# Reading packed zeros once per bit field, and moving small steps at the start of a dequantising FFN-attention-FFN kernel

## The reference

```python
def _dequant(qweight, scales, qzeros, g_idx):
    shifts = jnp.arange(PACK, dtype=jnp.uint32) * BITS          # PACK = 8, BITS = 4
    w = (qw[:, None, :] >> shifts[None, :, None] & MAXQ).reshape(-1, qweight.shape[1])
    z = ((qz[:, :, None] >> shifts[None, None, :] & MAXQ) + 1).reshape(qzeros.shape[0], -1)
    s = scales[g_idx]
    return (w.astype(scales.dtype) - z[g_idx].astype(scales.dtype)) * s
...
    h = jax.nn.silu(xf @ Wg) * (xf @ Wu)        # 512 -> 1376
    out = h @ Wd                                # 1376 -> 512
...
x = x + 0.5 * _L0_ffn_ref(_layernorm(x, axis=-1), ...)
x = x + _L0_attn_ref(_layernorm(x, axis=-1), ...)
x = x + 0.5 * _L0_ffn_ref(_layernorm(x, axis=-1), ...)
```

## Time and profile before

| | us |
|---|---|
| median of 3 runs | 819.42 (818.62 to 819.49) |
| the profiled execution | 819.34 |
| its span in the trace | 817.5 |
| TensorE busy in the span | 804.9 |
| VectorE / ScalarE / GpSimd busy | 497.4 / 271.3 / 303.5 |

### The profile page before, as it was taken

The page is one execution under the profiler, slowest core; times in us unless marked ns, Lnnn a source line. Parts: engine busy times, 40 slices in busy tenths (PEclk is TensorE's granted clock), DMA queues, the critical chain, the costliest instruction groups (busy, mean ns, idle before and its releaser), DMA issues.

```text
span 817.5 us, 10482 instructions
## 1 busy us (share of the span) xinstructions
PE 804.9 (98%) x3840; PEld 662.1 (81%) x3840; DVE 497.4 (61%) x801; ACT 271.3 (33%) x467; POOL 303.5 (37%) x237
## 2 busy tenths in 40 slices
PE   5999999999999999999999999999999999999998
PEld 4777788878888888788898888888878888888786
DVE  7999945756654543572869895545347743443452
ACT  3433423555211211342765862112124321221221
POOL 5655614751114463237554881055432110110100
PEclk9999999999999999999999999999999999999999
DMA  6999968965755368446366169554867164444131
GB/s 160 299 304 303 322 203 291 339 255 232 262 186 170 129 201 205 112 154 217 76 160 218 40 211 373 188 163 156 223 195 220 53 228 145 140 167 132 29 104 51
DMA packets 102301, 155.62 MB, mean 190 GB/s; under 512 B 51916, under 2 KB 62852, under 8 KB 97258
## 3 DMA queue, kind: packets, MB, share of 16 engines
q1 hardware_dynamic: 95056, 143.26, 54.2%
q10 hardware_dynamic: 6330, 7.47, 2.7%
q0 software_dynamic: 864, 4.23, 1.9%
HBM read 104.30 MB, written 44.27 MB: 182 GB/s over the span
## 4 chain that ended last, share of the span: by engine, by line
PE 93%; DVE 4%; issue 1%; DMA 1%; POOL 0%; ACT 0%; ACTq 0%; DVEq 0%
PE ps L896 44%; PE ps L889 39%; PE ps L951 5%; PE ps L970 2%; PE ps L1301 2%; PE ps L907 1%; DVE wi L1827 1%; DMA sc_gu<-in_L_ffn_up_scales 1%; DVE qs L1919 1%; PE ps L998 0%; DVE pT L1827 0%; DVE mx L2176 0%; DVE wf L1945 0%; DVE xT L1827 0%; ACTq L1637 0%
## 5 line engine op out<-in xcount | busy, mean ns | idle before, releaser
L889 PE MATMUL ps<-blk,ring 128*128 128x512 f32 (+1 forms) x1386 | 320.7, 389 | 0.0
L889 PEld LDWEIGHTS ps<-blk,ring 128*128 128x128 f32 (+1 forms) x1386 | 256.7, 185 | 57.8 <-issue 0.2
L896 PE MATMUL ps<-wd,hT 128*128 128x512 f32 (+1 forms) x963 | 227.7, 391 | 0.1
L896 PEld LDWEIGHTS ps<-wd,hT 128*128 128x128 f32 (+1 forms) x963 | 179.9, 188 | 38.7 <-DVE h L1995 0.5
L2403 POOL TENSOR_TENSOR h<-h,u 128x512 f32<-128x512 f32 (+1 forms) x33 | 42.7, 1294 | 299.4 <-ACT h L1558 299.4
L1830 DVE TENSOR_TENSOR u<-ps,p1s 128x512 f32<-128x512 f32 (+1 forms) x66 | 45.4, 687 | 95.5 <-PE ps L889 95.4
L1558 ACT ACTIVATE h<-h 128x512 f32<-128x512 f32 (+1 forms) x33 | 20.9, 632 | 174.9 <-DVE h L1830 174.9
L1830 DVE TENSOR_TENSOR h<-ps,p1s 128x512 f32<-128x512 f32 (+1 forms) x33 | 22.8, 691 | 64.1 <-PE ps L889 64.1
L1830 DVE TENSOR_TENSOR u<-ps,u 128x512 f32<-128x512 f32 (+1 forms) x66 | 45.6, 691 | 24.5 <-PE ps L889 23.4
L2344 POOL TENSOR_SCALAR xn<-xn,mv,rstd 128x512 f32<-128x512 f32 x28 | 59.0, 2114 | 0.8
L951 PE MATMUL ps<-xT,wp 128*128 128x512 f32 x240 | 58.6, 394 | 0.1
(11 more groups left out here) (145 smaller groups left out, 992.0 us busy)
## 6 DMA issues: line engine op xcount, KB each, us to landing
ring<-wsaved SPq DMA_DIRECT2D x29, 1024.0 KB, 5.2
ring<-wsaved SPq DMA_DIRECT2D x33, 768.0 KB, 4.5
wsaved<-wp SPq DMA_DIRECT2D x10, 1024.0 KB, 4.5
stream<-xres SPq DMA_DIRECT2D x32, 256.0 KB, 2.6
xres<-stream SPq DMA_DIRECT2D x32, 256.0 KB, 4.0
xn<-stream SPq DMA_DIRECT2D x7, 1024.0 KB, 7.3
wfull<-wf ACTq DMA_DIRECT2D x20, 256.0 KB, 4.9
wsaved<-wp SPq DMA_DIRECT2D x10, 512.0 KB, 5.2
```

What stands on the lines that cost most here:

```text
L889: mm = pe.matmul(ps[0:w, bank, :], ring[:, slot, which, a, kt, 0:w], blk[:, which, b, kt, :], start=not onto and kt == 0 and n == 0, stop= ...
L896: mm = pe.matmul(bank_ap, lhs(a), rhs(b), start=first and n == 0, stop=last and n == 2)
```

## The change

1. **Zeros.** The packed words are loaded with each word row on eight partitions (a broadcast over eight in the load), so gate and up take 64 partitions of 172 words and down 80 of 64. One shift by `shift`, a value per partition, replaces the eight shifts. The result lies field by field, so the two readers address it through a rearranged view: the zeros' multiplications of `scales_zeros` step 172 values (344 bytes) from one column to the next and the subtraction for down 64 values (128 bytes). `shift` is the first load of SP's stream, with a semaphore of its own; the zeros' loads follow it.
2. **Order in the head.** `ln_stats(0, (2, 3))` stands ahead of the first `ln_shift`, and the second `ln_shift` stands behind `table_gu` and `unpack(0)`.
3. **Less warming.** `keep_warm(2)` ahead of the first `scales_zeros` is gone, `keep_warm(4)` ahead of `plain_top` becomes `keep_warm(2)`.
4. **Attention, first sequence.** The low parts of the second tile of probabilities and of the values stand ahead of `ln_var(7)` and the low part of the queries; `pv` waits for five of s_qkvlo, and the score of tile 4 for six.

```diff
-            step(*(lambda j=j: eng.tensor_scalar(zi[:, :, j], zq, BITS * j, 15, ALU.logical_shift_right, ALU.bitwise_and)
-                   for j in range(PACK)))
-            step(*(lambda zb=zb, add=add, by=by: eng.tensor_scalar(zb, zi.rearrange("p c j -> p (c j)"), add, by, ALU.add, ALU.mult)
+            step(lambda: eng.tensor_scalar(zi, zq, shift[0:zq.shape[0], 0:1], 15, ALU.logical_shift_right, ALU.bitwise_and))
+            step(*(lambda zb=zb, add=add, by=by: eng.tensor_scalar(zb, zi, add, by, ALU.add, ALU.mult)
                    for zb, add, by in results))
...
+            sp.dma_start(shift[:, :], shifts).then_inc(d_shift, 16)
             for m in range(2):
-                sp.dma_start(zq_gu[m * ZP:(m + 1) * ZP, :], flat(zeros[m], ZC)).then_inc(d_zq_gu, 16)
-            sp.dma_start(zq_d, flat(zeros[2], ZC_D)).then_inc(d_zq_d, 16)
+                words = flat(zeros[m], ZC).rearrange("r (o c) -> r o c", o=1).to_broadcast([ZP, PACK, ZC])
+                sp.dma_start(zq_gu[m * ZP * PACK:(m + 1) * ZP * PACK, :], words).then_inc(d_zq_gu, 16)
+            sp.dma_start(zq_d, zeros[2].rearrange("r (o c) -> r o c", o=1).to_broadcast([GD, PACK, ZC_D])).then_inc(d_zq_d, 16)
...
-            sp.dma_start(shift[:, :], shifts).then_inc(d_small, 16)
...
+            def zeros_of(i, w):
+                words = slice(i * P // PACK, (i * P + w) // PACK)
+                return zb_gu[Z_ROWS, :].rearrange("r (j c) -> r c j", j=PACK)[:, words, :]
...
-                    pe.matmul(ps[:, Z_BANK, k * P:k * P + w], oh_gu[Z_ROWS, cols], zb_gu[Z_ROWS, i * P:i * P + w], start=True, stop=True)
+                    pe.matmul(ps[:, Z_BANK, k * P:k * P + w], oh_gu[Z_ROWS, cols], zeros_of(i, w), start=True, stop=True)
...
                 if r == 2:
-                    keep_warm(2)
...
-            keep_warm(4)
+            keep_warm(2)
...
+                            if j == 2:
+                                pe.wait_ge(s_qkvlo, 6)
...
-                        pe.wait_ge(s_qkvlo, 3 * (2 * b + 2))
+                        pe.wait_ge(s_qkvlo, 5)
...
+                    by_word = unit_view(u, z).rearrange("p (j c) -> p c j", j=PACK)
+                    minus(unit_view(u, wi[:, :]).rearrange("p (c j) -> p c j", j=PACK),
+                          flat.rearrange("p (c j) -> p c j", j=PACK), by_word).then_inc(s_int, 1)
...
+            ln_stats(0, (2, 3))
             ln_shift(0, (0, 1))
-            ln_stats(0, (2, 3))
...
-            ln_shift(0, (2, 3))
...
             unpack(0)
+            ln_shift(0, (2, 3))
...
+                p_lo(b, 1)
+                v_lo(a)
                 ln_var(t)
                 qk_lo(a, 0, qT)
-                p_lo(b, 1)
-                v_lo(a)
```

More of the change, by code:

```diff
@@ L204, in macaron @@
         left_gu = scratch("left_gu", [P, TAB_TILES * P], F32)
-        ZP = 16
-        ZC = GK * INTER // PACK // ZP
-        zq_gu = scratch("zq_gu", [P, ZC], I32)[0:2 * ZP, :]
-        zi_gu = scratch("zi_gu", [P, ZC, PACK], I32)[0:2 * ZP, :, :]
-        zs_gu = [scratch(f"zs_gu{m}", [P, ZC * PACK], BF16)[0:2 * ZP, :] for m in range(2)]
+        ZP = GK
+        ZC = INTER // PACK
+        zq_gu = scratch("zq_gu", [P, ZC], I32)[0:2 * ZP * PACK, :]
+        zi_gu = scratch("zi_gu", [P, ZC], I32)[0:2 * ZP * PACK, :]
+        zs_gu = [scratch(f"zs_gu{m}", [P, ZC], BF16)[0:2 * ZP * PACK, :] for m in range(2)]
         keep = scratch("keep", [P, 2], F32)
-        ZC_D = 8
-        ZP_D = GD * HID // PACK // ZC_D
+        ZC_D = HID // PACK
+        ZP_D = GD * PACK
         zq_d = scratch("zq_d", [P, ZC_D], I32)[0:ZP_D, :]
-        zi_d = scratch("zi_d", [P, ZC_D, PACK], I32)[0:ZP_D, :, :]
-        zb_d = scratch("zb_d", [P, ZC_D * PACK], BF16)[0:ZP_D, :]
+        zi_d = scratch("zi_d", [P, ZC_D], I32)[0:ZP_D, :]
+        zb_d = scratch("zb_d", [P, ZC_D], BF16)[0:ZP_D, :]
         over_blk = placer(blk_at, ring_at)
@@ L305, in macaron @@
         d_zb = sem("d_zb")
+        d_shift = sem("d_shift")
         d_cut_rest = sem("d_cut_rest")
@@ L521, in macaron @@
         FIRST_STEPS, PART_STEPS = 3, 7
-        ZERO_STEPS, ZERO_D_STEPS, TAB_STEPS = PACK + 2, 2 * PACK + 3, 2 * PACK + 4
+        ZERO_STEPS, ZERO_D_STEPS, TAB_STEPS = 3, 5, 6
         FLAT_LOADS, PART_LOADS = 32, 128
         def unpack_zeros(eng, step, zq, zi, *results):
-            step(*(lambda j=j: eng.tensor_scalar(zi[:, :, j], zq, BITS * j, 15, ALU.logical_shift_right, ALU.bitwise_and)
-                   for j in range(PACK)))
-            step(*(lambda zb=zb, add=add, by=by: eng.tensor_scalar(zb, zi.rearrange("p c j -> p (c j)"), add, by, ALU.add, ALU.mult)
+            step(lambda: eng.tensor_scalar(zi, zq, shift[0:zq.shape[0], 0:1], 15, ALU.logical_shift_right, ALU.bitwise_and))
+            step(*(lambda zb=zb, add=add, by=by: eng.tensor_scalar(zb, zi, add, by, ALU.add, ALU.mult)
                    for zb, add, by in results))
@@ L716, in _ @@
             for m, row in enumerate((Z_ROW, Z_UP)):
-                sp.dma_start(zb_gu[row:row + GK, :], zs_gu[m][m * ZP:(m + 1) * ZP, :]).then_inc(d_zb, 16)
+                sp.dma_start(zb_gu[row:row + GK, :], zs_gu[m][m * ZP * PACK:(m + 1) * ZP * PACK, :]).then_inc(d_zb, 16)
             sp.wait_ge(s_cst, 4)
@@ L1195, in turn_pair @@
                 turn_block(q, A12, kt)
-            pe.wait_ge(d_small, 32)
+            pe.wait_ge(d_small, 16)
             keep_warm(3)
@@ L1934, in dequantise @@
                     s, z = ps[:, S_BANKS[m], :], zeros_at(m)
-                minus(unit_view(u, wi[:, :]), flat, unit_view(u, z)).then_inc(s_int, 1)
+                    minus(unit_view(u, wi[:, :]), flat, unit_view(u, z)).then_inc(s_int, 1)
                 dve.wait_ge(s_int, u + 1)
@@ L2141, in _ @@
                 constants(lambda: dve.memset(keep[row:row + 2 * GK, 1:2], 0.0), lambda: dve.memset(keep[row:row + GK, 0:1], 0.0))
+            dve.wait_ge(d_shift, 16)
             dve.wait_ge(d_zq_gu, 32)
@@ L2158, in _ @@
             table_gu(dve, tables)
-            dve.wait_ge(d_small, 32)
             unpack(0)
+            ln_shift(0, (2, 3))
             dequantise(0)
```

## The result

The changed kernel takes 831.12 us (median of five runs, 830.63 to 831.75), the kernel before beside it 818.83 (818.44 to 819.49): a ratio of 1.0148, 95% interval 1.0137 to 1.0160. The forecast was 820.1 with a range to 823.0. The profiled execution took 830.63, its span is 828.7 where before has 817.5.

A forecast was written before the change was run, and what follows sets the result against it. TensorE, busy 804.9 of 817.5 us, was taken as the bound, leaving only its late start and few waits. Head +1.1, attention -0.3, reads and warming 0 gave +0.8 on 819.34: 820.1 us, range 817.9 to 823.0.

The forecast's parts named there:

- The strided reads: TensorE's 44 zeros' products and VectorE's 11 subtractions for down: stepped reads taken at nothing, with 2.4 us on TensorE as upper bound.
- the writing row: VectorE's eight old shifts of `zi_gu`, writing every 32 bytes, took 0.10 us apart for 43 words; read as steps being free.
- The rival that named this mechanism: Strided reads cost double: 2.4 us on TensorE beside the forecast's 0.8, 822.5 us; chance 0.18.
- The landing: When up's zeros arrive and VectorE's unpacking starts: 5.3 us instead of 3.56, bounds 4.1 and 6.3.
- the third load's 3.9 us: Landing time of `zq_d`, third in SP's stream before the change; it says 5.7 for up's zeros, and 5.3 was taken.
- The rest of the chain: Head: unpacking to second `nmr` 7.9 us, then 0.2 + 2.9 until ScalarE's stream is free for the first high part.
- the head's +1.1: ScalarE's first high part goes from 15.20 to 16.3, so TensorE's start and the weights' chain to 40.57 come 1.1 us later.
- Warming: Fewer multiplications ahead of `scales_zeros` and the first product: costed at nothing, since TensorE's four products wait for high parts anyway.
- a rival of 1.4 to 3.2 us: TensorE stays at 1.2 GHz longer for want of warming, 8 to 16 products slower: 822.4 with the rest; chance 0.12.
- Attention: TensorE's 0.42 us wait at 399.01 ends; late `ln_var(7)` delays GpSimd and ScalarE's third scaling, so 0.3 us gain is kept.
- the 1.2 us of VectorE that unpacking frees: One wide shift replaces eight in VectorE's head: 0.72 us freed for the first unpacking, 0.50 for down's.
- VectorE's step of 0.4 us being covered: VectorE's stepped subtraction for down: taken at nothing; upper bound 1.0 us for two down units ahead of 40.57, none hidden.

## Where the prediction was right and where it failed

**The strided reads: the step that failed most.** They were taken at nothing, "by the writing row", with an upper bound of twice the time, 2.4 us. They cost 7.0 to 7.2 us by the times and 5.9 in the trace (6.2 for the ten blocks, less 0.3 for the wait at 40.57, which is gone). The row chosen was a write, on another engine, and says nothing of a read by TensorE; the bound of two had no row behind it, and the factor was nearly four (0.20 for 0.055). The rival that named this mechanism was right in kind and had 0.18, but its price came from the same bound. With 0.15 x 44 = 6.6 added the sum would have been 826.7. The rule weighed beside it (the Trainium skill, "SBUF — State Buffer", section "Door 1: The DMA port swizzle") was right against the row; on TensorE two values to a 16-byte piece, with which it expects full rate, still cost nearly double (0.09 to 0.12 us for 0.055 to 0.07).

**The landing: mis-sized.** 5.3 was forecast, at most 6.3; it was 6.86. The step that failed is the term taken "a little less" than the third load's 3.9 us: from up's issue, at 2.10 and not 1.8, to unpacking it was 4.8. The forecast had weighed that four engines would carry this load, as its four marks bear out, and kept to the row. The rest of the chain held: from unpacking to the second `nmr` 7.84 us (forecast 7.9), from there to ScalarE's free stream 3.14 (3.1), the first high part at 17.88, where the same sum with 6.86 gives 17.86 (its bracket names VectorE's `wf`, but that was done by 17.0 and the stream at 17.84). So the head's +1.1 became 2.7 there by this one number. It is 2.4 at the first product and 2.8 at `scales_zeros(1)`: the four products between them took 2.10 us for 1.68, which no run here takes apart.

**Warming: the wrong case of the two.** It was costed at nothing with a rival of 1.4 to 3.2 us at 0.12. The rival came, 2.5 by the times, 2.0 in the trace. The argument against it was that nine microseconds of small products had not raised the level by 15 us. That is so, but the kernel before then rose at 18.2, just ahead of the 32 products, and some of the multiplications that the change took out were among the work in between; without them the changed kernel rose at 26.7.

**Attention: wrong sign.** The prediction named the very chain (`ln_var(7)` late, GpSimd full, the third scaling) and took 0.1 off for it; it took the whole 0.42 and 0.3 more.

With the four terms as the trace has them the sum nearly closes: 820.1, plus 5.9 for the reads, 1.7 for the head, 2.0 for the clock and 0.6 for the attention is 830.3; the profiled execution took 830.63, the median is 831.12.

**Right:** the 1.2 us of VectorE that unpacking frees (0.70 and 0.43), the small price of the order, and VectorE's step of 0.4 us being covered. The last was right by luck: its cover was TensorE's slowness, which the forecast did not have.

## What to carry to other kernels

A layout that saves a few instructions on an engine with time to spare must be priced by who reads it most often on the engine that has none: count the 16-byte pieces that each read of TensorE touches, and measure one such read if no row shows it. A bound without a row behind it is no bound. Before a step is put behind others, follow what it feeds, over GpSimd and ScalarE back to TensorE; and where a load is the first thing that the head waits for, look at what stands ahead of it in the stream: one more small load cost 1.6 us here, not the 0.5 of its issue. A clock that reads full is worth a check against the durations of equal instructions before a warming is taken out.

## What the chip showed that was not expected

- The zeros' products read bf16 at a price of about 1.6 to 1.8 ns for each 16-byte piece of a row touched; 128 values at steps of 16 to 344 bytes take 0.20 to 0.23 us, at 8 bytes 0.09 to 0.12, at 4 bytes nothing extra, and 0.20 at 1.2 GHz as well (21.41 to 21.61) as at 2.4. VectorE's reads are free up to 8 bytes and cost 0.4 us on 512 values from 16 bytes on.
- The views print a granted clock of 1.00 for the time ahead of a trace's first record, while the products may run at half rate (22.4 to 26.7 us in the changed kernel); the durations of equal instructions are the better witness there.
- Work at the very start of TensorE did not keep its clock up in either of two runs: the level fell again at 8.3 and 10.4 us, and the 32 products took 8.63 and 8.17 us.
- A load of four word rows puts four marks on its semaphore as its data lands, one of eight rows eight and one of sixteen rows sixteen. The wide loads' issues take 0.63 to 0.87 us for 0.40 to 0.42.
